# Token-first start order, an earlier deviation step and a merged shared-expert block in a two-layer fp32 transformer kernel

## The reference

```python
x = x + 0.5 * L0_ffn(layernorm(x))
x = x + L0_attn(layernorm(x))            # causal, 16 heads of 8
x = x + 0.5 * L0_ffn(layernorm(x))
x = x + 0.5 * L1_ffn(layernorm(x))       # top 2 of 8 experts
x = x + L1_attn(layernorm(x), ...)
x = x + 0.5 * L1_ffn(layernorm(x))
```

```python
aff = sigmoid(x @ Wr + br);  w = top 8 of 32, divided by their sum, 0 elsewhere
shared = (silu(x @ Wg_s + bg_s) * (x @ Wu_s + bu_s)) @ Wd_s + bd_s
routed = sum_e w[e] * ((silu(x @ Wg[e] + bg[e]) * (x @ Wu[e] + bu[e])) @ Wd[e] + bd[e])
```

## Time and profile before

| | us |
|---|---|
| median of 3 runs (lowest, highest) | 2148.38 (2147.45, 2151.19) |
| the profiled execution | 2147.88 |
| its span, first to last instruction | 2145.9 |
| PE busy | 2025.3 (94%) |
| DVE busy | 1644.6 (77%) |
| ACT busy | 1198.5 (56%) |
| POOL busy | 925.6 (43%) |

### The profile page before, as it was taken

The page is one execution under the profiler, slowest core; times in us unless marked ns, Lnnn a source line. Parts: engine busy times, 40 slices in busy tenths (PEclk is TensorE's granted clock), DMA queues, the critical chain, the costliest instruction groups (busy, mean ns, idle before and its releaser), DMA issues.

```text
span 2145.9 us, 44877 instructions
## 1 busy us (share of the span) xinstructions
PE 2025.3 (94%) x10800; PEld 1449.4 (68%) x10800; DVE 1644.6 (77%) x3338; ACT 1198.5 (56%) x1737; POOL 925.6 (43%) x904
## 2 busy tenths in 40 slices
PE   2999998999999999999999999998999999999999
PEld 2777777666666577777777777775333347777777
DVE  3777777777777667767758888886677788888887
ACT  3666664555555656666645444444667664454443
POOL 1655555232333356666644444442212234444444
PEclk9999999999999999999999999999999999999999
DMA  4333335223332134344411111112433411111111
GB/s 162 107 104 110 105 103 149 70 80 102 95 98 85 45 112 122 112 117 119 121 40 42 40 49 49 39 45 91 130 106 99 127 36 40 45 44 44 39 49 69
DMA packets 119981, 179.34 MB, mean 84 GB/s; under 512 B 33408, under 2 KB 37856, under 8 KB 119776
## 3 DMA queue, kind: packets, MB, share of 16 engines
q1 hardware_dynamic: 119904, 178.41, 27.5%
HBM read 147.15 MB, written 31.20 MB: 83 GB/s over the span
## 4 chain that ended last, share of the span: by engine, by line
PE 58%; issue 15%; POOL 13%; DVE 9%; ACT 2%; DMA 1%; POOLq 1%; DVEq 1%; SPq 1%; ACTq 0%
PE pair L389 12%; PE pair L391 12%; PE pair L390 11%; POOL h_lo L1305 9%; PE bank L611 4%; PE pair L697 3%; PE pair L719 3%; PE bank L589 2%; PE pair L780 2%; PE bank L389 2%; POOL rstd L1230 1%; DVE rmax L1134 1%; PE bank L391 1%; PE bank L390 1%; PE pair L706 1%
## 5 line engine op out<-in xcount | busy, mean ns | idle before, releaser
L1311 POOL TENSOR_TENSOR h_lo<-hid,h_hi 128x512 fp32r<-128x512 f32 x256 | 333.7, 1304 | 428.4 <-ACT h_hi L873 428.3
L389 PE MATMUL pair<-xnT_hi,w_hi 128*128 (+1 forms) x1056 | 433.2, 410 | 0.8 <-DVE prod L1057 0.8
L1305 POOL TENSOR_TENSOR h_lo<-hid,h_hi 128x512 fp32r<-128x512 f32 x256 | 329.8, 1292 | 228.6 <-ACT h_hi L841 227.3
L391 PE MATMUL pair<-xnT_hi,w_lo 128*128 (+1 forms) x1056 | 418.5, 396 | 0.0
L390 PE MATMUL pair<-xnT_lo,w_hi 128*128 (+1 forms) x1056 | 416.6, 395 | 0.0
L868 ACT ACTIVATE hid<-pair,bias 128x512 f32<-128x512 f32 x256 | 176.5, 689 | 328.1 <-PE pair L391 315.5
L389 PE MATMUL pair<-h_hi,w_hi 128*128 128x512 f32 x784 | 317.9, 405 | 19.1 <-POOL h_lo L1305 9.6
L391 PE MATMUL pair<-h_hi,w_lo 128*128 128x512 f32 x784 | 309.5, 395 | 0.0
L390 PE MATMUL pair<-h_lo,w_hi 128*128 128x512 f32 x784 | 308.2, 393 | 0.0
L1077 DVE TENSOR_SCALAR h_hi<-pair,nb 128x512 fp32r<-128x512 f32 x256 | 191.2, 747 | 83.6 <-PE pair L391 82.7
L1057 DVE SCALAR_TENSOR_TENSOR prod<-pair,bias,wb 128x512 f32<-128x512 f32 x256 | 191.0, 746 | 68.4 <-PE pair L391 55.7
(11 more groups left out here) (164 smaller groups left out, 3246.4 us busy)
## 6 DMA issues: line engine op xcount, KB each, us to landing
wb<-parts_dram SPq DMA_DIRECT2D x512, 128.0 KB, 2.8
wb<-parts_dram SPq DMA_DIRECT2D x128, 256.0 KB, 3.3
parts_dram<-attn_parts SPq DMA_DIRECT2D x96, 256.0 KB, 3.0
attn_q_st<-parts_dram SPq DMA_DIRECT2D x64, 256.0 KB, 2.7
k_one<-parts_dram SPq DMA_DIRECT2D x128, 64.0 KB, 2.4
attn_k_st<-parts_dram SPq DMA_DIRECT2D x32, 256.0 KB, 3.0
stage_w<-in_w_dram SPq DMA_DIRECT2D x32, 130.0 KB, 2.5
stage_w<-in_w_dram SPq DMA_DIRECT2D x6, 512.0 KB, 8.7
```

Source lines behind the costliest of these rows:

```text
L389: eng.matmul(o, w_hi_, v_hi, start=start, stop=False, **kw)
L391: return eng.matmul(o, w_lo_, v_hi, start=False, stop=stop, **kw)
L1305: eng.tensor_tensor(h_lo[:, p % NH0, :], hid[:, unit_of(p) % NHID, :] if p else hs[:, :], h_hi[:, p % NH0, :].bitcast(F32), ALU.subtract). ...
L1311: eng.tensor_tensor(h_lo[:, j % NH1, :], hid[:, j // 2 % NHID, :], h_hi[:, j % NH1, :].bitcast(F32), ALU.subtract).then_inc(lo1p_ready, 1)
```

## The change

1. **Start.** SP first loads chunk 0 of x (256 KB), the constants and then packed load 6, which holds the router's weights, then the biases and loads 2, 4 and 0; after these the rest of x and loads 1 and 3. Loads 5 and 7, row and the two scratch writes are issued after the router weights of chunk 0 are stored and its first 8 spreads are issued. ACT and DVE cut loads 0 to 3 (in the new order) between the steps of chunk 0's preparation, and the other four in slots 1, 3, 5, 7 (ACT) and 2, 4, 6, 8 (DVE) of the first body. PE waits for the loads that a block needs, in the first body alone.
2. **Deviation.** rstd goes from slot 2 to slot 1 in PREP["ffn0"], which serves the bodies of both ffn0 stages but the first body of the second one.
3. **Shared expert.** The 64 gate and 64 up columns lie side by side in one block of 128. PE computes three matmuls in slot 0 in place of six. silu of rows 0 to 63 is written to rows 64 to 127, hs has the product in rows 64 to 127 and the routing weights in rows 0 to 31. The down bias rows are loaded straight into the packed block, and stage_bd with its two operations goes.

```diff
 PREP = {
-    "ffn0": ((0, 1, 2, 3, 4, 6, 6, 7), (8, 8, 9, 9, 10, 11, 12, 12, 13, 15, 15)),
+    "ffn0": ((0, 1, 1, 3, 4, 6, 6, 7), (8, 8, 9, 9, 10, 11, 12, 12, 13, 15, 15)),
...
+LOAD_ORDER = (6, 2, 4, 0, 1, 3, 5, 7)
+LOADS_FIRST = {"act": {"hi": (0,), "lgT": (1,), "wT_out": (2, 3)}, "dve": {"lo": (0,), "top_a": (1,), "end": (2, 3)}}
+LOADS_LATER = {"act": {1: 4, 3: 5, 5: 6, 7: 7}, "dve": {2: 4, 4: 5, 6: 6, 8: 7}}
...
+        def cut_hi(eng, n):
+
+            _, hi, _, cols = loads[n]
+            eng.wait_ge(w_in[n % 4], 16 * sum(load_parts(m) for m in range(n % 4, n + 1, 4)))
+            eng.activation(hi, stage_w[:, n % 4, 0:cols], ACT.Copy).then_inc(w_hi_done, 1)
+
+        def cut_lo(eng, n):
+
+            _, hi, lo, cols = loads[n]
+            eng.wait_ge(w_hi_done, n + 1)
+            eng.tensor_tensor(lo, stage_w[:, n % 4, 0:cols], hi.bitcast(F32), ALU.subtract).then_inc(w_lo_done, 1)
...
         def pe_ffn0(eng, ch, p):
             base = ROUND + ch.g * NPS
             eng.wait_ge(hid_ready, base + reader(p, NGATE, NPS))
+            if ch.very_first:
+                eng.wait_ge(*loaded([GATE0 + unit_of(p), UP0 + unit_of(p)]))
...
-            eng.wait_ge(prod_ready, base + reader(p, 2, NPS))
-            products(eng, bank[2 + p % 2][:, :], w0_hi[:, UP0 + unit_of(p), :], w0_lo[:, UP0 + unit_of(p), :], xh, xl).then_inc(u_ready, 1)
+            if p:
+                eng.wait_ge(prod_ready, base + reader(p, 2, NPS))
+                products(eng, bank[2 + p % 2][:, :], w0_hi[:, UP0 + unit_of(p), :], w0_lo[:, UP0 + unit_of(p), :], xh, xl).then_inc(u_ready, 1)
...
+            if p == 0:
+                eng.activation(gate[own, :], gate_bank(p)[0:I0, :], ACT.Silu, bias=bias[0:I0, b:b + 1]).then_inc(silu_ready, 1)
...
-                eng.scalar_tensor_tensor(hs[0:I0, :], bank[2 + p % 2][0:I0, :], bias[0:I0, b:b + 1], gate[0:I0, :],
+                eng.scalar_tensor_tensor(hs[own, :], gate_bank(p)[own, :], bu_s[own, 0:1], gate[own, :],
...
+            eng.dma_start(x[:, 0:NT, :], x_in[:, 0:NT, :]).then_inc(x_in_sem, 16)
+            eng.dma_start(stage_c[:, :], consts[:, 0:C_SEL0]).then_inc(consts_in, 16)
+            load(0)
+            eng.dma_start(bias[:, :], biases).then_inc(bias_in, 16)
+            eng.dma_start(bu_s[own, :], biases[0:I0, BU + NP:BU + NP + 2]).then_inc(bias_in, 16)
+            for n in range(1, 4):
+                load(n)
+            eng.wait_ge(x_in_sem, 16)
+            eng.dma_start(x[:, NT:NB * NT, :], x_in[:, NT:NB * NT, :]).then_inc(x_in_sem, 16)
+            load(4)
+            load(5)
             store_weights(eng, Chunk(0, 0))
             for i in range(NWB):
                 spread(eng, Chunk(0, 0), i)
+            load(6)
+            load(7)
+            eng.dma_start(row[:, :, :], rows).then_inc(row_in, 16)
+            eng.wait_ge(zeroed, 2)
+            for i, src in enumerate((mixed_sb, mem0.aT)):
+                eng.dma_start(stacks[i, :, NROW * HD:PC, :], src[:, :]).then_inc(scr_w, 16)
```

More of the change, by code:

```diff
@@ L240, in build @@
         with ExitStack() as part:
+            stage_w = sb("stage_w", [P, 4, LOAD], F32, part)
+            stage_c = sb("stage_c", [P, C_SEL0], F32, part)
+        with ExitStack() as part:
             mem0 = AttnMemory("attn0", sb, part)
         w1_hi, w1_lo = sb("w1_hi", [P, NW1, P], F32R), sb("w1_lo", [P, NW1, P], F32R)
[L245 to L248, removed]
         with ExitStack() as part:
@@ L321, in build @@
                 loads.append((src[:, a:b], hif[:, a:b], lof[:, a:b], b - a))
+        loads = [loads[i] for i in LOAD_ORDER]
         areas = scratch.rearrange("g i h r s -> (g i h r s)").bitcast(F32).rearrange(
@@ L325, in build @@
         stacks, weights = areas[0], areas[1].rearrange("i h r s -> (i h) r s")
-        bd_rows = slice(I0, I0 + E0)
+        own = slice(I0, 2 * I0)
         w1_hif, w1_lof = (w.rearrange("p a b -> p (a b)") for w in (w1_hi, w1_lo))
@@ L410, in prep_table, with run @@
             return put + steps
-        def run(eng, who, prep, tail_, main, between=None):
+        def run(eng, who, prep, tail_, main, between=None, begin=None):
             def body(s, c):
@@ L427, in run @@
                 if engine == who:
+                    for n in LOADS_FIRST.get(who, {}).get(step, ()):
+                        cut_hi(eng, n) if who == "act" else cut_lo(eng, n)
                     prep(eng, step, Chunk(0, 0))
+            if begin is not None:
+                begin()
             for s in range(len(STAGES)):
@@ L456, in weight_rows @@
         def weight_rows(ch):
-            return (hs, bd_rows) if ch.kind == "ffn0" else (lgT, slice(0, E1))
+            return (hs, slice(0, E0)) if ch.kind == "ffn0" else (lgT, slice(0, E1))
         def weights_in(ch, i):
@@ L537, in pe_prep @@
             if step == "q":
+                if ch.first and ch.ga == 0:
+                    eng.wait_ge(w_lo_done, len(loads))
                 eng.wait_ge(xnT_lo_ready, ch.G + 1)
@@ L911, in dve_prep @@
                     eng.wait_ge(x_done, ONE + ch.G - NB + 1)
+                elif ch.very_first:
+                    eng.wait_ge(x_in_sem, 16)
+                elif ch.before().first:
+                    eng.wait_ge(x_in_sem, 32)
                 for t in range(NT):
@@ L1518, in _, with begin @@
                 eng.sem_inc(counts, ROUND)
[L1519 removed]
             for e in range(E1):
                 eng.memset(iota8[:, :, e], float(e)).then_inc(const_ready, 1)
[L1522 to L1530 removed]
+            def begin():
+                for n in LOADS_FIRST["dve"]["end"]:
+                    cut_lo(eng, n)
+                eng.wait_ge(bias_in, 32)
+                eng.tensor_scalar(nb1[:, :], bias[:, B1:B1 + NJ], -1.0, None, ALU.mult).then_inc(const_ready, 1)
             def ones(s):
@@ L1557, in main @@
                 if ch.kind == "ffn0":
+                    if ch.very_first and slot in LOADS_LATER["dve"]:
+                        cut_lo(eng, LOADS_LATER["dve"][slot])
                     dve_ffn0(eng, ch, slot)
```

82 lines of the change are left out of this document (46 added, 36 removed).

## The result

The changed kernel takes 2098.48 us (median of four runs, 2096.08 to 2099.55), the kernel before 2148.01 in the same session. The ratio is 0.9765, with a 95% interval of 0.9748 to 0.9782: 50 us less. The profiled execution took 2099.55, its span 2097.6.

The account below looks back on a forecast made before the run. PE, 94% busy, idles 31 us and waits for other engines in ffn0 bodies. Start 19.4, first-stage bodies 7.7, second-stage 8.9 and last body 0.4 sum to 36.4 us off 2147.88: 2111.5, range 2101 to 2122.

Parts of the forecast that it names:

- The start: Chunk 0's preparation: bn_stats at 3.9 in place of 27.69, hs near 18.4; 23.8 us gained.
- The first body: First ffn0 body 4.4 us longer: cuts +3.7, rstd -1.5, late wb +1.2, cuts blocked by POOL +1.0; bounds 1.9 to 8.
- The lock: First body: DVE's three cuts and POOL's h_lo block each other over SBUF; 0 to 3.9 us, taken as 1.0.
- the earlier rstd: First body: rstd in slot 1 takes away most of a 1.67 us wait, 1.5 us gained.
- Rival (c): First body worse: cuts and POOL block fully (+2.9), PE falls to its lower clock (about 3 us); 2117.5, chance 0.13.
- part 1: The new start less the longer first body: 23.8 - 4.4 = 19.4 us gained.
- The deviation: Looped first-stage ffn0 bodies: rstd in slot 1 ends the logits' wait for xnT_lo; 1.29 us each, 7.7 for six.
- Rival (d): Looped ffn0 bodies: the next wait takes the deviation's gain, a body gains only 0.6; 2121, chance 0.07.
- The second stage: Looped second-stage ffn0 bodies: 1.34 us from earlier logits plus 0.15 from earlier yT, 1.49 each, 8.9 for six.
- The merged block: Three matmuls fewer per ffn0 body, 0.70 us of PE work: 0 gained in the first stage, bounds 0 and 0.70.
- rival (b): Merged block pays too, since yT's chain has PE in it: 14 bodies x 0.70 = 9.8 us more, 2101.7; chance 0.14.

Follow-up runs that it names:

- a1_spare_before: Kernel before with one unused tile of 8 bytes per partition behind b2f, moving later tiles by 32 bytes: 2133.95 us, ratio 0.9937.
- a2_changed_unaligned: Changed kernel with an unused tile behind bu_s, so later tiles again stand 32 past a multiple of 64 bytes: 2108.03 us, ratio 0.9823.
- c3_two_cuts_early: Changed kernel with row and scratch writes issued before the router weights' store, and the fifth and sixth loads' DVE cuts in slot 1: 2099.29 us, ratio 0.9767.
- a3_rstd_in_slot_2: Changed kernel with rstd back in slot 2: 2110.93 us, ratio 0.9836 to the kernel before.
- a4_extra_up: Changed kernel with three unused up matmuls put back into slot 0 of each ffn0 body: 2096.05 us, ratio 0.9757 to the kernel before.
- b1_start_only: Changed kernel with rstd back in slot 2, three extra up matmuls in slot 0 and an unused tile behind bu_s: 2130.09 us, ratio 0.9913.
- c1_shift_64: Kernel before with 64 unused bytes per partition behind b2f: ratio 1.0002.
- b4_weights_at_64: Kernel before with two unused tiles, one ahead of the weights and one behind them: 2144.39 us, ratio 0.9986.
- d3_wa_as_xnT: Changed kernel with row and scratch writes before the router weights' store, and 64 unused bytes ahead of wa, 192 behind: 2097.26 us, ratio 0.9760.

## Why the prediction was wrong, point by point

**The step that failed** is a term that the sum did not have. The text costs bu_s nowhere. It took a new tile of 8 bytes per partition, and the new places of the tiles behind it, as free, and so had no bounds for it either. The measured worth is 13.5 us alone (a1_spare_before) and 12.5 us in the changed kernel: ratio 0.9765 against 0.9823 in a2_changed_unaligned, whose intervals do not touch. It is about 0.6 us in each ffn1 body, 0.3 in a looped body of the first ffn0 stage, next to nothing in the second. Without it the time would have been about 2110 (2148.01 x 0.9823; the run itself had 2108.03), inside the range and 1.5 to 3.5 us from the forecast. The trace of before could not have given the price: it has one placement, and nothing in it says what another would do. What could have been seen is that an edit in the list of tiles moves every tile behind it, and that the argument rested on the pace of 0.23 us staying as it was.

**The start** was right: 23.7 for 23.8, both marks within 0.1 us. (SP's issues to the end of load 3 are fourteen and not thirteen, done at 7.9 us, which cost nothing.) **The first body**: +4.08 for +4.4 in the changed kernel, +4.06 between the marks in a2_changed_unaligned (38.97 against 34.91). That the total came out so near is luck, since two of its parts were off and cancel. SP reached the spread for slot 5 when forecast (31.75, which is 55.4 less 23.7), but prod could start 4.2 us later and not 3.0, so DVE waits 2.00 us there, against 1.2 allowed (58.4 less 57.3 is 1.1). The lock went the other way: the three cuts took 1.21 or 1.22 us each, and it was POOL that stood still, its h_lo beside the cut at 31.32 taking 2.29 in place of 1.29. The Trainium skill (SBUF — State Buffer, Who interferes with whom) says that a VectorE instruction with two SBUF inputs and a GpSimd one that reads SBUF contend for ports that they share, and that the order of issue decides who is blocked. The trace agrees: the later starter pays, POOL 1.0 us there (it started 0.07 after the cut), DVE 0.7 us in c3_two_cuts_early (the cut at 24.15, beside an h_lo that had begun at 23.24). POOL had slack in the changed kernel, so the 1.0 us allowed for it was not lost on DVE. Nor are the parts independent, as the sum took them: what DVE does ahead of a wait for wb is swallowed by that wait. So the earlier rstd, put at 1.5 us here, was worth 0.24 (a3_rstd_in_slot_2).

**Rival (c)** was partly there. PE was at the lower level for a moment in that body, right behind its wait for the logits, and once more in the next, which the windows 40 to 48 and 72 to 76 of the changed kernel show as a granted clock of 0.73, 0.84 and 0.57. The last row below is a2_changed_unaligned's window 40 to 44:

```profile
40.00:44.00 4.00, 3.44 (x11) 2.71 (x12) 3.10 (x5) 2.75 (x5) 2.11 (x4) 0.73 0.35 110
44.00:48.00 4.00, 4.00 (x18) 2.90 (x17) 2.09 (x3) 3.42 (x5) 1.51 (x2) 0.84 0.28 91
...
72.00:76.00 4.00, 3.68 (x11) 3.02 (x12) 3.16 (x7) 1.39 (x4) 2.23 (x2) 0.57 0.41 133
...
40.00:44.00 4.00, 3.43 (x17) 2.59 (x17) 3.85 (x6) 2.96 (x5) 2.32 (x4) 1.00 0.31 106
```

In a2_changed_unaligned all windows from 20 to 120 us are at 1.00, and the two bodies are 1.0 and 1.7 us shorter (38.97 and 41.52 against 39.94 and 43.23), though its matmuls are the slower ones. It is not the address: the first of the two dips is there in a3_rstd_in_slot_2, a4_extra_up and b1_start_only as well (0.67, 0.64 and 0.57 from 40 to 44), and b1_start_only has the tiles where a2_changed_unaligned has them. The 19.4 for part 1 came out as 18.7 by the second mark in one and 19.7 in the other.

**The deviation** was right, 1.25 us for 1.29 in the first stage by a3_rstd_in_slot_2; so was the wait for yT that follows it, 0.95 for "about 1". Rival (d) fell. **The second stage** was right: 1.54 us a body for 1.49 in a2_changed_unaligned. In the first stage that kernel gains 1.04 for 1.29 forecast, so the 1.25 from the deviation holds nothing of the removed block, and some 0.2 us a body are lost elsewhere. b1_start_only has most of them too (40.38, against 40.24 before and 40.25 in c1_shift_64, which has the same places), so they came with the rest of the change; with which part of it stays open.

**The merged block** was right, at 0 in the first stage, by a4_extra_up. In the second stage it was put at 0.15 a body and is 0.07. This matters for how the result is read. With 2098.5 measured, the nearest case on record was rival (b), 2101.7, in which the merged block pays 0.70 in each body. Its mark was a body shorter by 2 us, and the bodies are shorter by 1.44; the putting back of the block settles it. A total near a rival's total is no evidence for the rival.

**What stays open.** Why the common remainder modulo 256 matters inside TensorE or SBUF is not shown. The runs show the relation and its price, not a mechanism, and whether it is the reads of moving data and weights that meet, or the writes of DVE, ACT and POOL into h and xnT, was not separated. With only h and weights alike the ratio is 0.9996 to 1.0005 at the four distances tried; the other two pairs were tried at one distance each, 0.9986 with only xnT and weights alike and 1.0026 with only xnT and h. The 0.9986 says that it is no matter of one matmul's own two operands alone: in b4_weights_at_64 xnT and the weights are alike, and the second matmul of a gate or up product still starts 234 ns behind the first, where it is 227 in the changed kernel.

## What to carry to other kernels

Any edit that adds, drops or reorders tiles moves all that come behind, and in a kernel bound by TensorE this alone was worth 0.6% here; cost it, and before crediting a change run the old kernel with the same shift. Where matmuls follow each other without a gap, try giving all moving tiles and weight tiles the same remainder modulo 256 bytes, and look at an untouched stage of the trace: if its bodies changed length, something other than the edit is at work. Work taken off an engine that is just about to wait is worth nothing, and work moved into a wait is worth nothing where the next wait takes it up, as c3_two_cuts_early shows.

## What the runs showed of the hardware that was not expected

- Matmuls of 512 columns start 227 ns apart or 227 to 236 depending on the addresses of xnT, the weights and h relative to each other modulo 256 bytes; 47.1 against 47.7 to 48.1 us for a body of 213 matmuls.
- A VectorE subtraction with two SBUF inputs and a GpSimd one that overlap don't share: the later starter is late by up to the rest of the other, GpSimd's by 1.0 us in the changed kernel (2.29 for 1.29), VectorE's by 0.7 (1.90 for 1.22) in c3_two_cuts_early.
- A store of 64 KB with 768 KB still in flight beside it let the next DMA start 3.8 us after it, where 1.7 us were enough without them (23.15 - 19.34 against 20.88 - 19.17); 4.1 and 4.6 us in the two other kernels with that order (d3_wa_as_xnT, c3_two_cuts_early).
- PE fell to its lower level behind waits of 1.3, 1.1 and 2.2 us in one body of the changed kernel, but not in a2_changed_unaligned, with 0.5, 1.3 and 2.2 us in the same places; and it fell in b1_start_only, with 0.8 and 2.2 us as the two last ones. The size of the waits alone does not say when it falls.
